# A four-layer attention kernel on one core: the last layer's order, one copy, one PSUM slot and the sums behind the first layer's denominators

## The reference

```
L0:  q, k, v = split(tokens @ w_proj + b_proj)            # 8 heads of 32
     attn = softmax(einsum('bihd,bjhd->bijh', q, k) * 32 ** -0.5, axis=j)
     x = (einsum('bijh,bjhd->bihd', attn, v)) @ w_out + b_out + tokens
L1:  group norm, one head of 256, softmax attention, wo, + x
L2:  mean/std norm, one head of 256, softmax attention, o_w, + x
L3:  kt = conv(x, w_qk); q, v from the 3x3-average-pooled x
     attn = softmax(kt over 16 channels) @ v, two mixtures weighted by pi
     out = batch_norm(conv(attn @ q, w_out)) + x              # over all images
```

## Time and profile before

| | us |
|---|---|
| median of 3 runs (2945.25 to 2949.44) | 2946.13 |
| the profiled execution, device time | 2946.01 |
| its span, first to last instruction | 2944.3 |
| TensorE busy, matmuls | 2645.1 |
| VectorE busy | 1984.8 |
| ScalarE busy | 1288.2 |
| GpSimd busy | 705.4 |

### The profile page before, as it was taken

How to read it: one execution, slowest core, us unless ns; L and a number is a source line. 1 busy time by engine, 2 the same in 40 slices (tenths; PEclk the granted TensorE clock), 3 DMA queues, 4 the chain that set the end, 5 groups by cost and what they waited for, 6 DMA issues and landing times.

```text
span 2944.3 us, 43959 instructions
## 1 busy us (share of the span) xinstructions
PE 2645.1 (90%) x15676; PEld 1842.3 (63%) x15676; DVE 1984.8 (67%) x2297; ACT 1288.2 (44%) x1874; POOL 705.4 (24%) x444
## 2 busy tenths in 40 slices
PE   5999999899898998989989899898998899898994
PEld 4447765477655775557755677456774477655772
DVE  2766677666875767666776677765777666876666
ACT  3453335533364433644346333463335533365333
POOL 0530035300371013600236002440035300362011
PEclk7899999999999998999999999899999999999997
DMA  4200041000500005000050002300032000500016
GB/s 125 65 15 1 12 100 37 16 1 11 136 1 16 1 11 136 2 16 1 29 119 1 16 12 56 81 2 15 12 76 61 16 1 12 119 18 1 1 44 281
DMA packets 46237, 123.51 MB, mean 42 GB/s; under 512 B 9904, under 2 KB 21424, under 8 KB 42416
## 3 DMA queue, kind: packets, MB, share of 16 engines
q1 hardware_dynamic: 46000, 120.36, 15.2%
HBM read 41.96 MB, written 23.86 MB: 22 GB/s over the span
## 4 chain that ended last, share of the span: by engine, by line
PE 80%; DVE 8%; ACT 5%; issue 5%; SPq 1%; DMA 0%; DVEq 0%; ACTq 0%
PE tile L1520 25%; PE pv L1520 11%; PE pv L1643 8%; PE tile L1605 8%; PE tile L1633 6%; PE tile L1766 4%; PE tile L1667 4%; PE pv L1633 2%; DVE small L1112 2%; PE pv L1896 2%; PE tile L1788 2%; PE tile L1817 2%; PE tile L1695 1%; PE tile L1678 1%; ACT p L845 1%
## 5 line engine op out<-in xcount | busy, mean ns | idle before, releaser
L1112 DVE TENSOR_REDUCE small<-tile 128x1 f32<-128x1024 f32 x512 | 600.8, 1216 | 174.9 <-PE tile L1605 174.7
L845 ACT ACTIVATE p<-tile 128x512 f32<-128x512 f32 (+1 forms) x632 | 405.5, 690 | 238.6 <-PE tile L1633 236.9
L1605 PE MATMUL tile<-stack 96*128 96x512 f32 x1024 | 370.9, 461 | 43.9 <-DVE small L1112 17.1
L736 POOL TENSOR_TENSOR row_sum<-act 128x256 f32<-128x256 f32 x32 | 41.6, 1318 | 1521.3 <-DVE act L1305 1521.3
L1520 PE MATMUL tile<-qk_r 128*128 128x512 f32 x1536 | 378.0, 395 | 0.0
L706 POOL TENSOR_TENSOR acc<-acc,p 128x1024 f32<-128x1024 f32 x144 | 339.5, 2388 | 0.6 <-ACT p L845 0.6
L1520 PEld LDWEIGHTS tile<-qk_r 128*128 128x128 f32 x1536 | 287.4, 188 | 66.4 <-issue 7.7
L1605 PEld LDWEIGHTS tile<-stack 96*128 96x128 f32 x1024 | 187.3, 204 | 225.0 <-issue 114.9
L1310 DVE TENSOR_TENSOR pl<-p,ph 128x1024 fp32r<-128x1024 f32 x128 | 158.2, 1236 | 221.0 <-ACT p L925 221.0
L1633 PE MATMUL tile<-stack 112*128 112x512 f32 x760 | 270.2, 424 | 14.7 <-DVE rec L1160 8.1
L1643 PE MATMUL pv<-p,v 128*32 128x512 f32 x2048 | 272.7, 606 | 1.4 <-ACT p L845 1.4
(11 more groups left out here) (282 smaller groups left out, 4450.5 us busy)
## 6 DMA issues: line engine op xcount, KB each, us to landing
stack<-qk_r SPq DMA_DIRECT2D x192, 256.0 KB, 5.1
x_in<-in_x_dram SPq DMA_DIRECT2D x8, 1024.0 KB, 5.0
act<-in_x_dram SPq DMA_DIRECT2D x8, 1024.0 KB, 4.9
x_scratch<-act SPq DMA_DIRECT2D x7, 1024.0 KB, 4.0
z_scratch<-act SPq DMA_DIRECT2D x7, 1024.0 KB, 6.5
stack<-ones SPq DMA_DIRECT2D x16, 256.0 KB, 5.9
w3f<-w3f_scratch SPq DMA_DIRECT2D x8, 512.0 KB, 3.2
fin_rest<-z_scratch SPq DMA_DIRECT2D x3, 1024.0 KB, 9.9
```

The lines of the kernel that those rows point to most:

```text
L845: sc.activation(p0[:, jt % DEPTH, pair, first:first + len(heads) * HALF], tile_wait(batch, "st0", *u, jt, k), ACT.Exp, scale=float(D) ** - ...
L1112: ve.tensor_reduce(maxima[:, h * NT + it:h * NT + it + 1], t, X, ALU.max).then_inc(vector_done, vector.one("max0", g, h, it))
L1605: ins = mm(o[:, s], stack[0:IMAX, g, 0, h, it * P:(it + 1) * P], stack[0:IMAX, g, 1, h, s], start=True, stop=True)
```

## The change

Sums: in the first three units key tiles 0 to 6 are added ahead of den0 (`SUMMED` 5 to 7): twelve adds a unit. Four of them, (jt, pair) in `BETWEEN`, go to VectorE, each behind the maxima of the key tile given there; the last one (`NT`) stands between the negations and max_rows. GpSimd keeps eight. den0 then sums `acc0` and key tile 7.

Last layer: mt, g, smt, z and the two tiles of the second head group's q and k (qk0(0,1), qk0(1,1)) are spread over the sixteen score tiles, some in halves; VectorE's block from the second window sum to sm moves behind the first max0, the mixing weights before the fourth; z's statistics move into key tiles 2 to 5 of unit (0,0); SP's `key_ones(1)` waits for qk0(1,1).

Copy: ScalarE's v0_kept(1) stands ahead of L2's q copies, v0_kept(0) behind the k copies. Slot: the ring of whole tiles starts at slot 0 for the last unit's first st0.

```
-SUMMED = 5
+SUMMED = 7
+BETWEEN = {(1, 1): 1, (3, 1): 4, (5, 1): 6, (6, 1): NT}
...
-    return "vector" if (g, half) == UNITS[-1] else "pool"
+    return "vector" if (g, half) == UNITS[-1] or (jt, pair) in BETWEEN else "pool"
...
+        if n == ("st0", *UNITS[-1], 0, 0):
+            rings[ring] = 0
...
-                if first:
-                    sp.wait_ge(tensor_done, tensor.at(n, "qk0", 1, 1))
-                else:
-                    sp.wait_ge(tensor_done, tensor.at(batch, "smt", 1))
+                sp.wait_ge(tensor_done, tensor.at(n, "qk0", 1, 1))
                 key_ones(1)
...
+                    if layer == 2 and not last:
+                        v0_kept(1)
                     for t in range(2):
...
-                            if (layer, t) == (2, 0) and not last:
-                                v0_kept(ct)
+                    if layer == 2 and not last:
+                        v0_kept(0)
...
+                    if last_unit(g, half):
+                        added(last_unit(g, half), NT)
                     t = tile_wait("m0", g, half)
...
+                def added(u, place):
+                    for (jt, pair), behind in BETWEEN.items():
+                        if behind == place:
+                            add0(u, jt, pair)
...
                 for k in range(G * HT):
-                    if body and k == 2:
+                    if body and k == 1:
+                        mixed_weights()
+                    if body and k == 3:
                         mixing()
-                    if body and k in (10, 13):
-                        z_stat((k - 10) // 3)
...
+                        if following:
+                            added(u, jt)
+                        if body and not former and jt in range(2, 2 + 2 * CT):
+                            z_stat(*divmod(jt - 2, 2))
...
-                    qk0(0, 1)
-                if body:
-                    mt_tile()
+                    qk0(0, 1, (0,))
                 for k in range(G * HT):
+                    if body and k == 1:
+                        mt_tile()
+                    if head and k == 2:
+                        qk0(0, 1, (1,))
                     if body and k == 2:
                         g_tile()
-                    if head and k == 2:
-                        qk0(1, 1)
-                    if body and k in (2, 4):
-                        smt_tile(k // 2 - 1)
-                    if body and k in (6, 9):
-                        z_tile(k // 3 - 2)
+                    if body and k in (4, 5):
+                        smt_tile(k - 4)
+                    if body and k in (7, 9, 12, 14):
+                        z_half(*((0, 0), (0, 1), (1, 0), (1, 1))[(7, 9, 12, 14).index(k)])
+                    if head and k in (10, 11):
+                        qk0(1, 1, (k - 10,))
                     if head:
                         s0(*rows_of(UNITS[0], k))
```

More of the change, by code:

```diff
@@ L218, in vector_steps @@
                 s += [("max0", *rows_of(following, 2 * jt + pair))] if following else []
-                s += [("add0", *u, jt - 1, pair)] if jt and adder(*u, jt - 1, pair) == "vector" else []
+                s += [("add0", *u, jt - 1, pair)] if not following and jt and adder(*u, jt - 1, pair) else []
+            s += [("add0", *u, *t) for t, behind in BETWEEN.items() if following and behind == jt]
+            s += [("z_stat", *divmod(jt - 2, 2))] if not last and jt in range(2, 2 + 2 * CT) else []
         if following:
             s += [(n, *following) for n in ("neg_hi", "neg_copy", "neg_lo")]
+            s += [("add0", *u, *t) for t, behind in BETWEEN.items() if behind == NT]
             s += [("max_rows", *following, h) for h in range(G // 2)]
@@ L1374, in softmax, with z_stat @@
                     TT(w, w, wide(wr), ALU.mult).then_inc(vector_done, vector.one("sm", k))
[L1376 to L1381, removed]
+                def z_stat(ct, k):
+                    dve.wait_ge(scalar_done, scalar.at(b, "z_kept", ct))
+                    row = slice(2 * b + k, 2 * b + k + 1) if last else bass.ds(2 * b + k, 1)
+                    ve.bn_stats(bn_rows[:, ct, row, :], (zlast if last else act)[:, ct, k * HALF:(k + 1) * HALF]
+                                ).then_inc(vector_done, vector.one("z_stat", ct, k))
                 head, body = not last, not first
@@ L1441, in turn @@
                     max_rows(*UNITS[0])
+                else:
+                    for ct in range(CT):
+                        z_stat(ct, 0)
+                        z_stat(ct, 1)
                 batch = b + 1
@@ L1590, in turn, with qk0 @@
                 kts = range(CT)
-                def qk0(t, g):
-                    o = free("qk0", t, g)
-                    for s in halves:
+                def qk0(t, g, parts=(0, 1)):
+                    o = free("qk0", t, g) if 0 in parts else where("qk0", t, g)
+                    for s in (halves[k] for k in parts):
                         ins = three(o[:, s], [[w[:, kt_, t, g * P:(g + 1) * P] for kt_ in kts] for w in (w0h, w0l)],
                                     [[x0[:, part, kt_, s] for kt_ in kts] for part in range(2)])
-                    ins.then_inc(tensor_done, tensor.one("qk0", t, g))
+                    if 1 in parts:
+                        ins.then_inc(tensor_done, tensor.one("qk0", t, g))
                 def s0(g, h, it):
@@ L1655, in den0 @@
                             pass
-                        elif (g, half) == UNITS[-1]:
-                            for pair in range(2):
-                                vector_wait("add0", g, half, jt, pair)
                         else:
                             for pair in range(2):
-                                pe.wait_ge(pool_done, gps.at(batch, "add0", g, half, jt, pair))
+                                if adder(g, half, jt, pair) == "vector":
+                                    vector_wait("add0", g, half, jt, pair)
+                                else:
+                                    pe.wait_ge(pool_done, gps.at(batch, "add0", g, half, jt, pair))
                         src = acc0[:, half] if jt < top else p0[:, jt % DEPTH]
```

48 lines of the change are left out of this document (26 added, 22 removed).

## The result

The changed kernel takes 2949.34 us (median of 20 runs) against 2944.66 for the kernel before in the same measurement: ratio 1.0015, 95% interval 1.0009 to 1.0022. It is slower by 4.7 us, where 2931, 15 faster, was forecast. The profiled execution took 2947.97 us (span 2946.1, granted clock 0.954, before 0.949).

A forecast was written before the change was run, and what follows sets the result against it. TensorE was taken as the bound (80% of the chain that ended last). Copy -14.8, slot -8.1, first units -14, units 2 and 3 +19, head 0 and +3 sum to -15: 2931 us, range 2918 to 2946.

The forecast's parts named there:

- I take 0 per batch (-6 to +3): Head: gain of 5 us at m0 offset by second-stack loads and lower clock; 0 per batch, +3 in the first.
- the 1.77 should stay: First unit of each batch: GpSimd is ahead of the exponentials, so the 1.77 us saved by 64 fewer products is kept.
- the slot: Last unit's first score tile no longer waits until VectorE has inverted the denominators: -8.1 us over eight batches.
- the copy: Layer 2: TensorE no longer waits before the key projection for ScalarE's copy of the second v0 tile: -14.8 us.
- -14: First units of eight batches: 1.77 us each saved by fewer denominator products, -14 us in all.
- Meetings of VectorE and GpSimd: Units 2 and 3: whichever engine's add comes second waits for the other's end; +1.2 us a unit, +19 us.
- the second stack: Head: moving qk0(1,1) later delays twelve loads that ScalarE's key tile 2 needs; 5 us gain becomes 1 to 3.
- (a): Rival: VectorE's adds fall between GpSimd's and meetings cost little, -1.77 us in every unit; 2884 us, chance 0.14.
- (b): Rival: second stack's loads are no bound, the head keeps its 5 us and the clock; 2875 us, chance 0.08.
- (c): Rival: VectorE becomes the bound of units 2 and 3, +3.0 us a unit; 2960 us, chance 0.18.
- (d): Rival: TensorE's wait of some 2.5 us before m0 lowers the clock at each boundary; 2987 us, chance 0.08.
- (e): Rival: nothing happens because the order on the engines stays what it was; 2946 us, chance 0.02.

The follow-up runs named there:

- sumsonly: Kernel before with only the sums changed (seven key tiles, four adds on VectorE): 2948.74 us, ratio 1.0015.
- copyslot: Kernel before with only ScalarE's copies moved in layer 2 and the last unit's slot changed: 2922.73 us, ratio 0.9927.
- short: early_nosums with key tiles 5 and 6 left out of the denominators of the first three units, no adds in their place: 2843.20 us, ratio 0.9661.
- late_first: early_z0 with VectorE's first add moved behind the maxima of key tile 2 instead of key tile 1: 2921.14 us, ratio 0.9922.
- early_thin: early with GpSimd's adds of key tiles 2 to 6 cut to 8 of 1024 columns, VectorE's adds whole: 2870.88 us, ratio 0.9748.
- early_six: early with six key tiles summed, all ten adds of a unit on GpSimd, none on VectorE: 2977.31 us, ratio 1.0112.
- early: Changed kernel with qk0(1,1) moved back ahead of z, at the sixth and seventh score tile: 2921.59 us, ratio 0.9924.
- early_z0: early with z's four statistics at the first unit's key tiles 0 and 1 instead of 2 to 5: 2906.44 us, ratio 0.9873.
- nosums: Changed kernel with the old sums (five key tiles, all eight adds on GpSimd in the first three units): 2942.30 us, ratio 0.9994.
- early_nosums: early with the old sums (five key tiles, adds on GpSimd alone): 2900.56 us, ratio 0.9848.
- tail: early with six key tiles summed, GpSimd keeping its old eight adds, VectorE doing two between negations and rows of the maxima: 2869.03 us, ratio 0.9747.

## Why the prediction was wrong

The step that failed is **"I take 0 per batch (-6 to +3)"** for the head, with "the 1.77 should stay" for the first unit's adds. By the starts in all eight batches, head and first unit together lost 40 us; forecast were 3. The other terms held, and where they missed, they missed towards faster: the three later units with the slot won 7.4 (forecast 3.1), the copy 17 (14.8), the norm 11 and the end of the kernel some 3 (both 0). The "-14" is counted here with the later units: a unit's spared products stand behind the next m0, and sumsonly shows 14 us of them in the fourth units. In the first unit nothing was there to offset what its adds cost. That the time came out within 5 us of the kernel before is luck, a balance of 38 us won and 40 lost.

- **The copy, the slot, the products**: right, shown by copyslot and short.
- **Meetings of VectorE and GpSimd**: right. Whoever comes second waits for the other's end. By the prediction's chain units 2 and 3 take 31.8 us (its own steps add up to 31.6); they took 31.5, m0 waiting for the negations as forecast, 1.3 us in place of 2. Of the chain's three meetings the first held VectorE 1.3 us (forecast 1.4), with 1.2 us of TensorE's behind it through `res` where I had 0.6; the second didn't happen; the third held it 1.85 (2.4). Late_first and early_thin show that the holds, not the added work, make most of the cost. The Trainium skill ("SBUF — State Buffer", section "SBUF: two separate sides") has a GpSimd operation and a VectorE one with two SBUF inputs, or in a mode that takes both ports, block each other for the whole instruction of the one that comes first. Late_first's 3.40 us agrees: 1.22 and less than one GpSimd add. Early_six's 4.24 goes beyond it, over more than one add.
- **The first unit**: wrong, and three terms make its +8.0 us. sumsonly shows 2.2 from the adds, which meet GpSimd there too: that GpSimd is ahead of the exponentials in this unit doesn't keep it idle when VectorE comes. early against sumsonly shows 2.1 more, and early_z0 gives 1.65 of them back by moving z's statistics alone: each was set against a gap of 0.72 us, but the adds and their holds had taken those gaps already, and with the statistics in front of it the third add came behind the start of one more GpSimd add (2.66 us in early, 1.44 in sumsonly). I spent the same gap twice. after against early shows 3.7 from the second stack. The three add up because each is taken from the run before; in another order their sizes differ, as the next point shows.
- **The second stack**: the mechanism was right (the wait for the loads is there, eight times, 34 us), its size too small. qk0(1,1) was done 1.6 us later than worked out (ScalarE starts on it at 1144.19). The last load landed 1.4 us later after its issue than the 2.2 of the first batch, which the prediction's "up to 22" allowed: from ScalarE's start to tile 2 it took 21.8. The 4.6 us from ScalarE to SP's first load came exactly. So tile 2 won 0.4 where 1 to 3 were forecast, m0's 3.8 us were lost again before it, and ScalarE waited 4.0 us where about 7 were named as the sign. By nosums against early_nosums the late stack alone costs 4.8 us of unit 1 in this batch: with the gaps still there, the unit catches up on none of ScalarE's 4.3 us of waiting.
- **The head itself** (qv to m0) won 2.2 to 3.8 us a batch, short of the 5 that the schedule gave. Early's head is 1.9 shorter than sumsonly's in every batch; how much of that is the statistics' place and how much the new order, no run separates.
- **Rivals**: (a), no cost of the meetings, is out by the adds of 2.51 and 3.07 us. (b), the stack being no bound, is out by ScalarE's eight waits for it. (c) came true in the first unit, where I hadn't put it: VectorE is the bound there. (d) played no part: the 1.27 us waits before m0 left the granted clock at 1.00 in unit (0,1). (e), 2946, came nearest to the time, but its reason did not hold: the stages moved by up to 8 us.

```profile
1152.48:1189.60 37.12, 30.48 (x133) 15.44 (x134) 30.01 (x29) 18.98 (x37) 18.90 (x8) 0.86 0.47 124
1189.60:1221.10 31.50, 28.67 (x198) 14.88 (x198) 29.35 (x28) 19.17 (x38) 23.04 (x10) 1.00 0.02 7
```

In these windows (columns as in the earlier trace rows) the first unit's VectorE is busy for 30.01 us, holds included, up from 20.65. The granted clock of the whole unit, 0.86 against 0.88 before, hides that it fell a second time, behind ScalarE's wait. The first two rows are the changed kernel, the third is the kernel before, from its own tile 2 on:

```profile
1166.00:1170.00 4.00, 3.39 (x13) 1.59 (x14) 0.90 (x3) 2.03 (x4) 2.77 (x2) 0.69 0.00 0
1170.00:1174.00 4.00, 4.00 (x20) 2.34 (x19) 3.36 (x4) 2.52 (x5) 4.00 (x2) 0.88 0.02 4
1168.00:1172.00 4.00, 4.00 (x26) 2.00 (x19) 2.87 (x3) 2.53 (x5) 4.00 (x3) 1.00 0.00 0
```

From 1168 to 1170 us it was 0.50. So the restart at the lower level of 1.2 GHz, which the prediction named, took place. By these rows it is worth at most an estimated 1.7 us of the 8.0 (the missing 0.31 and 0.12 of 4 us each); no run separates it from the wait itself.

## What to carry to other kernels

A gap on an engine is a budget: write each gap down once and strike it out when a part of the change uses it, before the parts are summed. An add of two SBUF tiles given to VectorE isn't parallel work while GpSimd stays busy with its own (late_first, early_thin); find the stretch in which GpSimd has ended, and put VectorE's there (tail), and keep GpSimd's own run away from VectorE's short operations on the path. When a producer is moved later in an order, follow its data to the last consumer: here twelve loads stood between a matmul and an exponential.

## What was not expected of the hardware

- **A short VectorE operation waited through two GpSimd adds.** In early_six a negation of 128 x 16, one input, stood 4.24 us, across the rest of one GpSimd add and all of the next (six of them ran without a pause). So it did not get its turn when the first add ended. It was seen there only; elsewhere the negations take 0.17.
- **GpSimd is held too**: its longest add in the changed kernel took 3.41 us, where 2.43 was the longest before (2.39 the median in both). The changed kernel's row, in ns (min/median/max):

```profile
L714 POOL TENSOR_TENSOR acc<-acc,p x168: 2347/2386/3408, 106.2 to 2668.8; 128x1024 f32<-128x1024 f32 x168
```
- **A stall of TensorE at the start of a loop's turn.** Ahead of the second group-norm product TensorE stood 1.4 to 2.6 us in the six batches whose turn begins with a jump back, and some 0.5 in the first and the last. The long wait was there in every run whose first three units sum four sources by products (before, copyslot, nosums, early_nosums), with 147 instruction transfers in the trace. It was in none of the others (132 to 138), short among these, which differs from early_nosums in TensorE's program alone. The transfers on the page of before, then of short:

```profile
q8 instruction: 147, 2.41, 0.3%
q8 instruction: 132, 2.16, 0.3%
```

Without the wait the norm of the changed kernel is about 11 us shorter over the eight batches; some 9 are the wait itself. The Trainium skill ("Runtime: NRT & Kernel Launch", section "Instruction fetch mechanics") has a taken branch stall for the fetch of its target, if that isn't loaded yet. The six batches fit that, though the wait stands some products behind the start of the turn. Why fewer products a unit end it stays open: whether the length counts or where the jump's target lies wasn't tried.
